# A pause between indirect gathers on GpSimd in place of a lock to the run sums, in a graph and mixture-of-experts layer

## Chip, cores and metric

The kernel runs on one core of one Trainium2 chip. The metric is the device time of one execution in microseconds (us). The time before is the median of three runs.

## What is computed

There are 6250 nodes of 256 float32 features, a first graph of 200,000 edges sorted by their target `dst`, and a second graph of 131,072 edges for a gate that picks two of four experts. Cut to what matters:

```python
x = x + gnn(_layernorm(x), W, M, src, dst)
x = x + ffn(_layernorm(x)[None], ...)[0]

def gnn(x, W, M, edge_src, edge_dst):
    self_term = x @ W
    msg = x @ M
    agg = segment_sum(msg[edge_src], edge_dst, num_segments=x.shape[0])
    return relu(self_term + agg)
# ffn: graph attention over edge_index gives scores (B, N, 4); top 2 are weighted by softmax;
#      out += g[..., None] * (gelu(x @ W1[e] + b1[e]) @ W2[e] + b2[e]) for e in range(4)
```

## The kernel before

The change lies in the first graph. The message product is taken after the sum, so what has to be summed over edges is the normalized `x` itself, kept in DRAM as `xn_d`. The sorted edges are cut into 1611 **visits** (`V_`): one visit is 128 edges whose targets lie in one tile of 128 nodes. For each visit j

- GpSimd (POOL in the profile) issues an indirect gather that fetches the 128 source rows of 1 KB each from `xn_d` into one slot of `ring` (line 1703);
- TensorE (PE) multiplies the slot by a 128 x 128 `one_hot` matrix of local targets, made on VectorE (line 752), which sums the rows by target in PSUM (line 1505);
- VectorE (DVE) adds that sum to the running sum of the tile and writes it back over the slot (line 818). This is `run`, with its place in VectorE's count of steps, `dve_at["run", j]`. The PE may be three visits ahead of it, no more: the matmul of visit j waits for `run` of visit j - 3.

`ring` has `RING = 4` parts of `JC = 8` slots. Eight visits are a **chunk**. When a chunk's run sums are done, the queue of SyncE (SP) stores it to `run_d` (line 1885), on a semaphore `stored{s}` of its part. TensorE waits at the start of a chunk until all eight gathers of it have landed. GpSimd may begin the gathers of chunk c when the chunk four places back is stored and the run sum of visit 8(c - 3) is done, so at most 24 visits ahead of the run sums. Before the change a second rule is in force: every even gather j waits also for the run sum of visit j - 14 (`LEAD = 14`).

Between visits, TensorE, VectorE and ScalarE (ACT) do other work in an order written out by hand and counted by visits: the sort of the second graph's edges (`sort_after`), the experts' matmuls (`unit_after`), and per tile of nodes the layer's product, its norm and its gate features (`due`). SP's queue moves the tiles of those. So a visit that comes later moves all of them. GpSimd does nothing but gathers in this stage. After the last visit GpSimd scatters the starts of the second graph's segments, and the second graph, which takes the rest of the time, begins.

Of the kernel before, what the change touches and what calls it, by code (L numbers as in the profile page):

```python
# [3 lines left out]
F32 = mybir.dt.float32  # L4
# [8 lines left out]
P = 128  # L13
# [14 lines left out]
UNIT_LAG = 2  # L28
LATE = 2
EARLY_STARTS = 27  # L30
LEAD = 14

TC = 32
WIDE_CHUNKS = 3
# [31 lines left out]
def sent(k):  # L66

    return 16 * (k + 1)


def build(nc, x, src, dst, W, M, W_gat, att_src, att_dst, b_gat, ln_gamma, ln_beta,
# [81 lines left out]
    r = Region(base)  # L153
# [20 lines left out]
    shift1 = r.take("shift1", [P, P], F32)  # L174
    up1 = r.take("up1", [P, P], F32)
    wrap1 = r.take("wrap1", [P, P], F32)
    node_id = r.take("node_id", [P, NT], F32)
    node_ii = r.take("node_ii", [P, NT], I32)
    row_at = r.take("row_at", [P, 1], I32)
# [135 lines left out]
    V, S, T, G, Q = nc.vector, nc.scalar, nc.tensor, nc.gpsimd, nc.sync  # L315
# [3 lines left out]
    def sem(name):  # L319
        if name not in named:  # L320
            named[name] = nc.alloc_semaphore(name)
        return named[name]

    dve_step = sem("dve_step")
    dve_at = {}

    def at_rows(ap):
        return bass.IndirectOffsetOnAxis(ap=ap, axis=0)
# [35 lines left out]
    def size(c):  # L364

        return max(0, min(JC, V_ - c * JC))
# [1293 lines left out]
    def gpsimd_program():  # L1660
# [32 lines left out]
        for c in range(NCH):  # L1693
            s = c % RING
            if c * JC % P == 0:
                G.wait_ge(sem("sources"), c * JC // P + 1)
            if c >= RING:
                G.wait_ge(sem(f"stored{s}"), sent(c // RING - 1))
                G.wait_ge(dve_step, dve_at["run", (c - RING + 1) * JC])
            for j in range(c * JC, c * JC + size(c)):  # L1700
                if j % 2 == 0 and j >= LEAD:
                    G.wait_ge(dve_step, dve_at["run", j - LEAD])
                G.indirect_dma_start(out=ring[:, s, j % JC, :], out_offset=None, in_=xn_d,  # L1703
                                     in_offset=at_rows(srci[:, j:j + 1])).then_inc(sem(f"gather{s}"), 16)

# [25 lines left out]
        for c in range(NCF):  # L1731
# [3 lines left out]
            for k in range(pool_cols[c]):  # L1735
                j = c * FC + k
# [250 lines left out]
    scalar_program()  # L1987
    tensor_program()
    gpsimd_program()
    sync_program()  # L1990

# [21 lines left out]
```

## Time and profile before

| what | value |
|---|---|
| median of 3 runs | 4055.15 us (4053.32 to 4062.95) |
| the profiled execution, its own time | 4024.76 us |
| its span, first to last instruction | 4023.5 us |
| granted TensorE clock, mean | 0.823 of full speed |
| first and last gather of the first graph | start at 63.8 and 2525.2 us |
| POOL gathers of the first graph | 1611, mean 973 ns |
| POOL busy over the span | 2164.3 us (54%) |

The first graph's visits fill 2461 us of the span (63.8 to 2525.2), over 60% of it. A group row gives the busy time of all its instructions, the mean time of one, and after the second bar the idle time of its engine right before them with what ended it. On POOL, spans of an instruction are rough, so the distance from start to start is the surer figure. "Issue" is idle time that no semaphore of the profile ended. PE and PEld (weight loads) are two rows of one engine, so their waits overlap.

### The profile page before, as it was taken

To read this page: it belongs to the slowest core of one execution; us is meant where nothing else is said; L and a number is where in the kernel's file an instruction comes from. 1 tells how busy PE (TensorE), PEld (TensorE's weight loads), DVE (VectorE), ACT (ScalarE), POOL (GpSimd) and SP (SyncE) were. 2 spreads that over 40 slices of the span, in tenths; PEclk is the share of its full clock that TensorE was granted. 3 is DMA by queue.
4 is the path that set the end of the run, shared out by engine and by line. 5 is a ranking of instruction groups with operands and counts; after the bars stand their busy time and mean duration, and the time that the engine had idled before them with its cause. 6 is when DMAs were issued, how large, how long until landed. Compare 5 with 4: busy or idle time off the path is not lost. (4 is left out here: it accounts for less than half of the span.)

```text
span 4023.5 us, 43371 instructions
## 1 busy us (share of the span) xinstructions
PE 2676.5 (67%) x13459; PEld 1995.0 (50%) x13459; DVE 2157.3 (54%) x5820; ACT 903.1 (22%) x1563; POOL 2164.3 (54%) x2248
## 2 busy tenths in 40 slices
PE   2567867776677776877877877622694646555844
PEld 1344545554455455555555555401683535454844
DVE  6777667776655556554545555200263534344866
ACT  3001111111122221111111111100352423233633
POOL 4666666666666665666666666577014353534031
PEclk9767879898888888999899888755896867777978
DMA  9676656666666665666666666401221111111146
GB/s 298 207 253 189 195 182 201 202 195 190 191 202 198 194 191 173 206 204 199 209 195 208 209 202 194 112 13 14 64 70 27 45 27 32 39 26 36 44 138 203
DMA packets 476804, 601.22 MB, mean 149 GB/s; under 512 B 72486, under 2 KB 415390, under 8 KB 474526
## 3 DMA queue, kind: packets, MB, share of 16 engines
q1 hardware_dynamic: 378766, 375.94, 28.6%
q0 software_dynamic: 97216, 219.88, 20.0%
q10 hardware_dynamic: 592, 2.64, 0.2%
q8 instruction: 108, 1.77, 0.2%
q14 instruction: 122, 1.00, 0.1%
HBM read 313.06 MB, written 286.79 MB: 149 GB/s over the span
## 5 line engine op out<-in xcount | busy, mean ns | idle before, releaser
L1703 POOL DMA_INDIRECT ring<-xn_d,srci x1611 | 1567.2, 973 | 902.1 <-DVE ring L818 416.9
L1505 PE MATMUL wide<-ring,one_hot 128*128 128x256 f32 x3222 | 983.1, 442 | 470.5 <-DVE ring L818 351.7
L818 DVE SCALAR_TENSOR_TENSOR ring<-ring,same_v,wide 128x256 f32<-128x256 f32 x1610 | 770.3, 478 | 942.6 <-remote 405.9
L1505 PEld LDWEIGHTS wide<-ring,one_hot 128*128 128x128 f32 x3222 | 666.5, 218 | 740.8 <-DVE ring L818 318.4
L1611 PE MATMUL wide<-tab_parts,low_hot 128*128 128x208 bf16 x6288 | 659.9, 262 | 329.5 <-issue 308.7
L1737 POOL DMA_INDIRECT g<-tab_d,srt x500 | 480.8, 962 | 629.5 <-DMA sum_d<-g 480.4
L1611 PEld LDWEIGHTS wide<-tab_parts,low_hot 128*128 128x128 bf16 x6288 | 576.3, 100 | 413.2 <-issue 377.0
L1563 PE MATMUL wide<-w2s,hh 128*128 128x256 f32 x1568 | 424.8, 420 | 150.5 <-issue 88.5
L1563 PEld LDWEIGHTS wide<-w2s,hh 128*128 128x128 f32 x1568 | 335.5, 216 | 225.9 <-issue 102.8
L1553 PE MATMUL wide<-xt,w1s 128*128 128x512 f32 (+1 forms) x832 | 419.1, 631 | 41.2 <-ACT hh L1238 23.5
L1238 ACT ACTIVATE hh<-wide,b1c 128x512 f32<-128x512 f32 (+1 forms) x208 | 137.7, 663 | 1299.1 <-remote 627.3
L875 DVE TENSOR_TENSOR picked<-wide,high_hot 128x832 f32<-128x832 f32 x131 | 133.8, 1021 | 466.7 <-remote 380.5
L752 DVE TENSOR_SCALAR one_hot<-iota_f,dloc 128x128 f32<-128x128 f32 x1611 | 363.0, 304 | 6.2 <-remote 3.0
L1314 ACT ACTIVATE low_hot<-far_off,ones 128x512 bf16<-128x512 f16 x262 | 173.9, 711 | 488.8 <-remote 418.2
L1553 PEld LDWEIGHTS wide<-xt,w1s 128*128 128x128 f32 x832 | 174.5, 216 | 174.3 <-issue 132.6
L793 DVE TENSOR_TENSOR yo<-wide,b2b 128x256 f32<-128x256 f32 x196 | 82.2, 419 | 270.5 <-remote 169.0
L1308 ACT ACTIVATE far_off<-low_row,lane_n 128x512 f16<-128x512 f16 x262 | 172.5, 706 | 0.0
L880 DVE TENSOR_REDUCE g<-picked 128x64 f32<-128x832 f32 x131 | 133.7, 1020 | 4.5
L1204 ACT ACTIVATE signs<-wide,smt 128x512 bf16<-128x512 f32 x98 | 67.3, 687 | 295.5 <-remote 151.8
L1257 ACT ACTIVATE tin<-wide 128x512 f32<-128x512 f32 x49 | 29.2, 596 | 389.8 <-remote 238.6
L650 DVE TENSOR_TENSOR keys<-keys 128x512 f32<-128x512 f32 (+1 forms) x198 | 112.2, 566 | 0.0
L651 DVE TENSOR_TENSOR keys<-keys 128x512 f32<-128x512 f32 (+1 forms) x198 | 112.1, 566 | 0.0
(369 smaller groups left out, 1730.2 us busy)
## 6 DMA issues: line engine op xcount, KB each, us to landing
run_d<-ring SPq DMA_DIRECT2D x201, 1024.0 KB
ring<-xn_d,srci POOLq DMA_INDIRECT x1611
y_d<-yo SPq DMA_DIRECT2D x196, 128.0 KB
comb<-y_d SPq DMA_DIRECT2D x28, 896.0 KB, 10.5
low_row<-low_d SPq DMA_DIRECT2D x13, 1024.0 KB
sum_d<-g SPq DMA_DIRECT2D x15, 768.0 KB, 3.9
g<-tab_d,srt POOLq DMA_INDIRECT x500
xn_d<-ring SPq DMA_DIRECT2D x7, 896.0 KB, 7.0
```

What stands on the lines that cost most here:

```text
L752: dve_at["one_hot", b] = step(V.tensor_scalar(one_hot[:, b % 4, i, :], iota_f[:, :], dloc[:, 4 * b + i:4 * b + i + 1], None, ALU.is_equal))
L818: dve_at["run", j] = step(V.scalar_tensor_tensor(out=o, in0=ring[:, (j - 1) // JC % RING, (j - 1) % JC, :], scalar=same_v[:, j:j + 1], in1 ...
L875: dve_at["taken", b] = then(V.tensor_tensor(picked[:, :, :, :], wide[:, 4 + half:6 + half, :].rearrange("p c (k x) -> p (c k) x", k=2)[:, ...
L1238: A.activation(hh[:, i % 2, f, 0:n * P], bank[hidden_bank[nl]][:, 0:n * P], ACT.Gelu, bias=b1c[:, e, f:f + 1], scale=1.0).then_inc(sem("ge ...
L1308: A.activation(far_off[:, b % 2, i, :], low_row[:, c % 2, at:at + LOW], ACT.Abs, bias=lane_n[:, 3 - i:4 - i]).then_inc(sem("far_off"), 1)
L1314: A.activation(low_hot[:, b % 2, 3 - i, :], far_off[:, b % 2, i, :], ACT.Relu, bias=ones[:, 0:1], scale=-1.0).then_inc(sem("low_quarter"), 1)
L1505: T.matmul(wide[:, 4 + j // 2 % 2, j % 2 * D:(j % 2 + 1) * D], one_hot[:, j // 4 % 4, j % 4, :], ring[:, j // JC % RING, j % JC, :], start ...
L1553: mm = T.matmul(bank[hidden_bank[nl]][:, 0:n * P], w1s[:, e, k, f * P:(f + 1) * P], xt[:, c % 2, k, 0:n * P], start=(k == 0), stop=(k == K ...
L1563: mm = T.matmul(bank[y_bank[ny]][:, 0:D], hh[:, i % 2, k, f * P:(f + 1) * P], w2s[:, e, k, :], start=(k == 0), stop=(k == KF - 1))
L1611: mm = T.matmul(bank[4 + 2 * (b % 2) + i // 2][:, at:at + HX * HI], low_hot[:, b % 2, q_, i * P:(i + 1) * P], tab_parts[:, k, q_, :, :].re ...
L1703: G.indirect_dma_start(out=ring[:, s, j % JC, :], out_offset=None, in_=xn_d, in_offset=at_rows(srci[:, j:j + 1])).then_inc(sem(f"gather{s} ...
L1737: G.indirect_dma_start(out=g[:, s, k, :], out_offset=None, in_=tab_d, in_offset=at_rows(srt[:, j:j + 1])).then_inc(sem(f"feat_in{s}"), 16)
```

## The change

Before each of the 1611 gathers, GpSimd writes zeros to a new tile `pause` of 128 x 128 float32, which nothing reads. The wait of every even gather for the run sum fourteen visits back is removed. Each memset waits until the one before it has completed, a memset that stands in GpSimd's order ahead of the gather ahead of it. The rules of the ring (part stored, run sum 24 visits back) stay, and now hold the chunk's first memset.

```diff
-LEAD = 14
+PAUSE = 128
...
     wrap1 = r.take("wrap1", [P, P], F32)
+    pause = r.take("pause", [P, PAUSE], F32)
...
                 G.wait_ge(sem(f"stored{s}"), sent(c // RING - 1))
                 G.wait_ge(dve_step, dve_at["run", (c - RING + 1) * JC])
             for j in range(c * JC, c * JC + size(c)):
-                if j % 2 == 0 and j >= LEAD:
-                    G.wait_ge(dve_step, dve_at["run", j - LEAD])
+                if j >= 1:
+                    G.wait_ge(sem("paused"), j)
+                G.memset(pause[:, :], 0.0).then_inc(sem("paused"), 1)
                 G.indirect_dma_start(out=ring[:, s, j % JC, :], out_offset=None, in_=xn_d,
                                      in_offset=at_rows(srci[:, j:j + 1])).then_inc(sem(f"gather{s}"), 16)
```

The other engines' programs keep their instructions and their order. GpSimd's order before, at the start of the gathers: `pairs` is an earlier gather, `ring<-xn_d,srci` are the visits' gathers.

```order
L1689 DMA pairs<-pair_d,vis_at 128x256 x12
L1703 DMA ring<-xn_d,srci 128x256 [waits xn_out3,xn_out2,sources,xn_out1,xn_out0]
L1703 DMA ring<-xn_d,srci 128x256 x13
L1703 DMA ring<-xn_d,srci 128x256 [waits dve_step]
L1703 DMA ring<-xn_d,srci 128x256
L1703 DMA ring<-xn_d,srci 128x256 [waits dve_step]
```

Fourteen gathers stand without a wait on VectorE's count, and from then on every second one has one. In the changed kernel the same place of GpSimd's order reads:

```order
L1690 DMA pairs<-pair_d,vis_at 128x256 x12
L1704 MEMSET pause 128x128 [waits xn_out3,xn_out2,sources,xn_out1,xn_out0]
L1705 DMA ring<-xn_d,srci 128x256
L1704 MEMSET pause 128x128 [waits paused]
L1705 DMA ring<-xn_d,srci 128x256
```

Memset and gather alternate, and VectorE's count is no longer waited for. Further on in the changed kernel, at visit 32, where the first part of the ring is used again, GpSimd's order reads:

```order
L1704 MEMSET pause 128x128 [waits paused,dve_step,stored0]
L1705 DMA ring<-xn_d,srci 128x256
L1704 MEMSET pause 128x128 [waits paused]
L1705 DMA ring<-xn_d,srci 128x256
L1704 MEMSET pause 128x128 [waits paused]
```

The wait for the ring's part now stands once in eight gathers, on the memset, and is the only one on another engine.

## Rows read from the trace of the kernel before

**Rows 1.** The profile's page: busy times, then TensorE's clock and DMA by slices

```profile
span 4023.5 us, 43371 instructions
PE 2676.5 (67%) x13459; PEld 1995.0 (50%) x13459; DVE 2157.3 (54%) x5820; ACT 903.1 (22%) x1563; POOL 2164.3 (54%) x2248
POOL 4666666666666665666666666577014353534031
PEclk9767879898888888999899888755896867777978
DMA  9676656666666665666666666401221111111146
```

**Rows 2.** Busy time of each engine in the stretch of the visits

```profile
core 0: us, PE busy (x) PEld busy (x) DVE busy (x) ACT busy (x) POOL busy (x), PEclk, DMA share, GB/s
63.00:2530.00 2467.00, 1822.38 (x6506) 1285.69 (x6507) 1472.04 (x4375) 403.71 (x679) 1569.25 (x1614) 0.86 0.65 202
```

**Rows 3.** Groups of instructions on POOL: gathers, and the start's memsets of 128 columns

```profile
L1703 POOL DMA_INDIRECT ring<-xn_d,srci x1611 | 1567.2, 973 | 902.1 <-DVE ring L818 416.9 <-issue 394.0 <-DVE one_hot L752 58.6
L1672 POOL MEMSET ones<- 128x128 f32 x1 | 0.2, 199 | 0.0
L1671 POOL MEMSET up<- 128x128 f32 x1 | 0.2, 198 | 0.0
```

**Rows 4.** Timeline of POOL, gathers one behind another: start, us, idle before

```profile
165.60 1.14 POOL L1703 DMA_INDIRECT ring<-xn_d,srci  x1 [0.30 <-issue]
167.05 0.94 POOL L1703 DMA_INDIRECT ring<-xn_d,srci  x1 [0.30 <-issue]
168.30 0.94 POOL L1703 DMA_INDIRECT ring<-xn_d,srci  x1 [0.30 <-DVE ring L818]
169.55 1.19 POOL L1703 DMA_INDIRECT ring<-xn_d,srci  x1 [0.30 <-issue]
```

**Rows 5.** The gathers' line: duration (min/median/max, ns), first and last start

```profile
L1703 POOL DMA_INDIRECT ring<-xn_d,srci x1611: 942/949/1807, 63.8 to 2525.2; - x179
```

**Rows 6.** The gathers alone by stretches: length, busy (count), clock, DMA share, GB/s

```profile
63.00:205.00 142.00, 99.41 (x100) 0.79 0.76 245
205.00:353.00 148.00, 98.75 (x100) 0.68 0.74 233
353.00:660.00 307.00, 197.46 (x197) 0.86 0.62 190
2200.00:2530.00 330.00, 205.14 (x216) 0.88 0.67 204
```

**Rows 7.** The visits' matmul, L1505: what ended the idle time before it

```profile
  DVE ring L818: 670.1, 338
  issue: 304.5, 294
  DMA ring<-xn_d,srci: 135.2, 62
```

**Rows 8.** Waits of the whole core: who waited for whom, total, times, longest

```profile
PEld wide L1505 <- DMA ring<-xn_d,srci: 70.8, 36, 5.4
PE wide L1505 <- DMA ring<-xn_d,srci: 64.4, 26, 15.3
DVE ring L818 <- remote: 405.9, 102, 8.4
DVE ring L818 <- PE wide L1505: 326.0, 175, 8.5
```

**Rows 9.** VectorE's `one_hot` line, and four of them in the timeline

```profile
L752 DVE TENSOR_SCALAR one_hot<-iota_f,dloc x1611: 267/281/515, 67.0 to 2527.0; 128x128 f32<-128x128 f32 x179
L752 DVE TENSOR_SCALAR one_hot<-iota_f,dloc 128x128 f32<-128x128 f32 x1611 | 363.0, 304 | 6.2 <-remote 3.0
1701.60 0.90 DVE L752 TENSOR_SCALAR one_hot<-iota_f,dloc 128x128 f32<-128x128 f32 x4
```

## Prediction

> **What bounds the kernel now.** I read the page first: TensorE is busy 67% of the span, VectorE and GpSimd 54% each, the DMA engines about 0.6 in the first graph's part [rows 1]. Nothing there is full, so the stretch of the visits was read next: of 2467 us TensorE is busy 1822 (74%), VectorE 1472 (60%), GpSimd 1569 (64%), DMA 0.65 [rows 2]. The visits are a loop over three engines, and what it lacks must be looked for in its waits.
>
> GpSimd's row says how the 1611 gathers share their time: 1567.2 us busy and 902.1 idle before them [rows 3]. The timeline shows what that idle time is made of: even where GpSimd waits for no one there are 0.30 us between the end of one gather and the start of the next, so the shortest distance from start to start is 1.25 us (168.30 to 169.55) [rows 4]. 1611 x 0.30 = 483 us are this gap, and 902 - 483 = 419 us are real waiting, 0.26 us for each gather. Most of it is put down to the run sum, 416.9 us (of which each of its 305 times holds the gap of 0.30 too); the `one_hot` that is named after it counts on the same semaphore [rows 3]. GpSimd is therefore not the bound: it could do a gather in 0.973 + 0.30 = 1.27 us and is asked for one in (2525.2 - 63.8) / 1610 = 1.529 us [rows 5].
>
> Who asks? TensorE's idle time before the visits is 670.1 us for the run sum, 304.5 "issue", and only 135.2 for the gathers' data [rows 7]. That last figure adds two rows of one engine, 70.8 us before weight loads and 64.4 before matmuls [rows 8], which may overlap; so late data cost somewhere between 71 and 135 us of TensorE's time at the very most, and the loop between TensorE and VectorE costs several times that. VectorE in its turn waits 326.0 us for the visits' matmul and 405.9 for a release that the trace does not name [rows 8]. The two stand in each other's way, and a gather earlier or later changes that only through the 71 to 135 us.
>
> **The change, part by part.**
>
> *The lock goes.* It removes the 419 us of waiting, but not as time won: GpSimd's waiting is where the loop is slower than GpSimd. What it brings is lead. With the lock the last pair of gathers of a chunk (8c + 6 and 8c + 7) may start only when the run sum of visit 8c - 8 is done, while TensorE wants the chunk when about the run sum of 8c - 3 is done: five visits, 5 x 1.53 = 7.6 us, less two gathers (2.5 us), leave 5.1 us for the transfer, and less where TensorE catches up after a wait. Without it only the ring's rule is left, 24 visits back, checked once in eight gathers. The late data of 71 to 135 us should then nearly vanish. How much of it is won? TensorE set free there runs sooner into its wait for the run sum of three visits back, the largest wait it has (670.1). I take half of the smaller figure, 35 us; the bounds are 0 and 71.
>
> *The memset comes.* The trace has memsets of exactly this shape at the start, 198 and 199 ns each, one right behind the other with no idle time [rows 3]. None of them stands behind a gather, so the price there is bounded. From below it is 0: the 0.30 us gap might be GpSimd's preparation of the next gather, and the memset might run within it. From above it is 0.199 + 0.30 = 0.50 us, if each change between memset and gather costs a gap again. I take 0.199, added to both the gather and its gap, because the memset's row shows no gap of its own. The pace is then 0.973 + 0.30 + 0.199 = 1.472 us a gather, 1611 x 1.472 = 2371 us for all, against 2461 now. The memset eats 321 of the 419 us that the lock took; GpSimd keeps 90 us of slack, 4%. The wait for the memset before is met already, since that one ran ahead of a whole gather, and costs nothing. If the slack is gone, every further 0.01 us of pace costs 16 us.
>
> *The places where GpSimd is the bound all the same.* The first hundred gathers take 142 us and the second hundred 148 [rows 6], 1.42 and 1.48 us each; at 1.472 the first hundred take 5 us more, the second about as now. The first chunk of eight lands 8 x 0.2 = 1.6 us later. From 353 on the gathers run at 307 / 197 = 1.56 us, and at the end at 330 / 216 = 1.53 [rows 6], slower than the new pace, so the ring fills and GpSimd waits for stores. Together 7 us lost, bounds 2 and 15.
>
> *VectorE beside the memset.* A `one_hot` takes 281 ns in the median and 515 at most, 304 in the mean [rows 9]; gathers go from 949 in the median to 1807 [rows 5]. The two disturb each other already. 1611 more writes of GpSimd might stretch some VectorE instructions by a part of 0.2 us; if one in five is hit by 0.1 us that is 32 us of VectorE's time, of which its 40% of idle time hides most. I set 6 us, bounds 0 and 32.
>
> Sum, against the profiled execution's own 4024.76 us: -35 + 7 + 6 = -22, so 4003. The medians of the runs shown stand 1.0076 times above it, so 4055 x (4003 / 4025) = 4033 us. Everything after the last visit keeps its work and is moved as a whole.
>
> **The rivals.**
>
> *A, the data were never the bound (no change, 4055).* The 71 us come back as waits for the run sum, and the start's 7 us are hidden. For it: 670.1 us of such waits against 135.2, and 405.9 us on VectorE that no gather ends. Against it: one wait of a matmul for the data is 15.3 us long [rows 8], and such a wait moves everything behind it.
>
> *B, the pause makes GpSimd the bound (slower).* The point from which this decides is a pace of 1.529 us. `one_hot` fills 363.0 of 2461 us, 15% of the time, in packs of four that last 0.90 us [rows 9]. If a memset that meets such a pack is held until it ends, it waits 0.45 us in the mean, 0.15 x 0.45 = 0.07 us a gather, and the pace is 1.54: 1611 x 1.54 = 2481 us, 20 more than now. GpSimd still waits for the ring now and then, a tenth of today's waiting by my guess, 42 us, less the 35 won and with the 6 on VectorE: 20 + 42 - 35 + 6 = 33 more, about 4088. For it: single gathers of 1.14 and 1.19 us in rows [rows 4] show that GpSimd is held now and then. Against it: the mean of 973 is only 24 ns over the median, so gathers, four times as long, lose little by all of VectorE's work.
> The Trainium skill, SBUF — State Buffer, section Who interferes with whom, states the rule that would do this: VectorE in a mode with two ports and GpSimd share one pair of ports, and whoever comes second is blocked for the whole instruction. That the gathers' mean lies so close to their median speaks for a small effect.
>
> *C, a gap of 0.30 us before the memset as well as before the gather (much slower).* The pace is 0.973 + 0.30 + 0.199 + 0.30 = 1.77 us; 1611 x 1.77 = 2854, 393 us more than now, about 4450. For it: the gap of 0.30 stands before every gather, also where nothing is waited for. Against it: no memset has one.
>
> *D, the memset hides in the gap.* The pace stays near 1.27 us, nothing is lost at the start, GpSimd runs ahead until the ring is full, and the gain is 35 to 71 us, about 4010. Against it: gathers come in denser bursts than any now, on DMA engines that are 0.65 busy, and could delay the other transfers; then it is no gain at all.
>
> **How the numbers follow.** My forecast (4033, own range 4010 to 4048) has 0.45, A 0.20, B 0.17, C 0.06, D 0.12. From no change this measurement can tell about 0.3%, 12 us. Faster by more than that: most of the forecast (0.33), two thirds of D (0.08), a little of A (0.02), together 0.43. Slower: all of C (0.06), most of B (0.14), small parts of the others (0.06), 0.26. The same: the rest, 0.31. The range reaches from D and a full gain of 71 us with nothing lost to B at its dearer end with a pace of 1.55 (2497 us, 36 more, plus the ring's 42): 3990 to 4110. Outside it are C and what lies below, about 0.12.
>
> **What would show it.** In the changed kernel's trace: the distance from gather to gather in an undisturbed stretch at 1.45 to 1.50 us (D: 1.27, C: 1.75); memsets of about 199 ns; TensorE's wait for the gathers' data down from 135.2 to under 30 us, after the first 200 us; GpSimd waiting mostly once in eight, for the store or the run sum; the last gather's start near 2505 us. Wrong I would be if distances above 1.53 fill the stretch and GpSimd hardly waits for anyone (B), or if the wait for data falls and the wait for the run sum grows by as much (A). A change in how long VectorE waits for what the trace does not name (405.9 us) would mean that the spacing of the gathers acts on something that I have not priced.

## The result and the profile after

The changed kernel is slower: 4263.89 us in the median of four runs (4257.78 to 4281.76) against 4059.05 us (4053.32 to 4069.32) for the kernel before in the same round, a ratio of 1.0509 (95% interval 1.0468 to 1.055). The forecast was 4033 us, and 4264 lies outside its range, between rivals B and C and by the mechanism of neither. The profiled execution of the changed kernel took 4269.35 us.

The page of the changed kernel, its busy times and the rows of slices:

```profile
span 4268.1 us, 44957 instructions
PE 2691.5 (63%) x13434; PEld 2006.0 (47%) x13459; DVE 2159.6 (51%) x5820; ACT 904.4 (21%) x1563; POOL 2540.3 (60%) x3859
POOL 5777777777776766676677677567502535353121
PEclk9667988797887888888888888875598677768878
DMA  9576565565564655555565556621131111111146
```

Beside [rows 1], no engine became fuller except GpSimd, whose 376 us more are nearly all memsets (368.9). TensorE, VectorE and ScalarE do the same work in a longer time. The slices, each 107 us long here and 101 before, keep their shape: the visits end in the 26th in both. What lies behind the last gather takes 4268.1 - 2757.1 = 1511 us, and took 1498.

The groups on POOL and VectorE in the changed kernel: busy time, mean of one, then the idle time before them and what ended it:

```profile
L1705 POOL DMA_INDIRECT ring<-xn_d,srci x1611 | 1577.7, 979 | 282.4 <-issue 269.7 <-POOL pause L1704 9.6 <-DVE ring L819 1.3
L1704 POOL MEMSET pause<- 128x128 f32 x1611 | 368.9, 229 | 476.3 <-DMA run_d<-ring 426.8 <-issue 27.1 <-DVE one_hot L753 12.9
...
L819 DVE SCALAR_TENSOR_TENSOR ring<-ring,same_v,wide 128x256 f32<-128x256 f32 x1610 | 770.9, 479 | 1172.4 <-remote 602.2 <-PE wide L1506 362.7 <-issue 105.7
L753 DVE TENSOR_SCALAR one_hot<-iota_f,dloc 128x128 f32<-128x128 f32 x1611 | 364.8, 313 | 3.4 <-DVE keys L652 0.2
```

Against [rows 3] the gathers lost their wait for the run sum and kept only a short gap. What GpSimd waits for now is the ring's part, 426.8 us for the store `run_d` before the first memset of a chunk. So GpSimd still has time to spare, and it is not the bound.

The gathers' own line, duration, first and last start:

```profile
L1705 POOL DMA_INDIRECT ring<-xn_d,srci x1611: 954/955/6902, 63.8 to 2757.1; - x179
```

The last gather starts at 2757.1 us in place of 2525.2 [rows 5], 231.9 us later. That is nearly the whole difference of the two profiled executions, 4269.35 - 4024.76 = 244.6 us. A visit takes (2757.1 - 63.8) / 1610 = 1.673 us instead of 1.529.

The chain of waits of the whole core names the place, in the changed kernel:

```profile
DVE ring L819 <- remote: 602.2, 127, 14.3
DVE ring L819 <- PE wide L1506: 362.7, 193, 8.5
DVE ring L819 <- issue: 105.7, 40, 14.0
```

"Remote" is the profile's word for a release that it can't name. VectorE waits for it 602.2 us where it waited 405.9 [rows 8], 196.3 us more, half of it by more waits (127 for 102) and half by longer ones (14.3 us at most, 8.4 before). All of VectorE's idle time before the run sum went from 942.6 to 1172.4 us, 230 more, nearly the 231.9 that the stretch grew; the rest of it, 36.7 us, is waiting for the visits' matmul. When both kernels were run again (below), the split was less sharp: of a stretch 214 us longer, 126 us were the unnamed waits (458.9 to 584.8) and 61 us the waits for the matmul.

One of these waits, in the timelines of the changed kernel (start, duration, then the idle time before), first VectorE, then TensorE, then GpSimd:

```profile
1777.20 1.05 DVE L819 SCALAR_TENSOR_TENSOR ring<-ring,same_v,wide 128x256 f32<-128x256 f32 x2
1791.24 1.06 DVE L819 SCALAR_TENSOR_TENSOR ring<-ring,same_v,wide 128x256 f32<-128x256 f32 x2 [12.99 <-remote]
...
1778.40 1.10 PE L1506 MATMUL wide<-ring,one_hot 128*128 128x256 f32 x4 [0.30 <-DVE ring L819]
1792.37 2.08 PE L1506 MATMUL wide<-ring,one_hot 128*128 128x256 f32 x4 [12.86 <-issue]
...
1779.49 0.22 POOL L1704 MEMSET pause<- 128x128 f32 x1
1779.88 0.95 POOL L1705 DMA_INDIRECT ring<-xn_d,srci  x1 [0.17 <-issue]
1780.82 0.23 POOL L1704 MEMSET pause<- 128x128 f32 x1
1781.22 0.95 POOL L1705 DMA_INDIRECT ring<-xn_d,srci  x1 [0.17 <-issue]
...
1789.26 0.95 POOL L1705 DMA_INDIRECT ring<-xn_d,srci  x1 [0.17 <-issue]
1790.21 0.22 POOL L1704 MEMSET pause<- 128x128 f32 x1
1790.60 0.95 POOL L1705 DMA_INDIRECT ring<-xn_d,srci  x1 [0.17 <-issue]
```

The matmuls that VectorE needs are recorded as over at about 1779.5 us (their ends are modelled, so this is rough). VectorE sees it at 1791.24, and TensorE, three visits ahead, can't go on either. All that time GpSimd issues one gather every 1.34 us. I call such a wait a **hold**: work of TensorE that is over reaches its waiters microseconds late.

Could it be VectorE itself that is kept from starting, while the news is there? The trace says no. It also keeps the times at which semaphores were counted up. In this example the semaphore of the visits' matmuls, which only TensorE counts, is recorded at 1776.29 and then at 1791.22 us, and at least 600 of the 602.2 us end on a count of this semaphore. Not every count is recorded, but these times agree with VectorE's start. ScalarE has unnamed waits of its own, nearly all behind other semaphores that only TensorE counts (of the first row, 485.3 us lie in the visits' stretch; the second lies there whole):

```profile
ACT hh L1239 <- remote: 683.7, 52, 33.0
ACT signs L1205 <- remote: 248.2, 39, 13.4
```

Holds are in the kernel before too, but shorter. This is one of its timelines, VectorE and then GpSimd:

```profile
1712.50 2.23 DVE L818 SCALAR_TENSOR_TENSOR ring<-ring,same_v,wide 128x256 f32<-128x256 f32 x4 [4.96 <-remote]
...
1709.57 0.95 POOL L1703 DMA_INDIRECT ring<-xn_d,srci  x1 [0.30 <-issue]
1713.24 0.95 POOL L1703 DMA_INDIRECT ring<-xn_d,srci  x1 [2.73 <-DVE ring L818]
```

Here the lock did something that the prediction had not seen. No run sum is done during a hold, so GpSimd soon runs into the lock; it fell silent at 1710.52 us, and the hold ended at 1712.50. With the lock gone GpSimd may go on until the ring is full.

Does the silence end the hold? I counted the unnamed waits at the run sum of 3 us or more. In the two traces of the kernel before, 145 of 158 ended while GpSimd had been idle for more than 0.6 us, with about 2 us of idle time in the median. The count proves little, since the lock opens only when the hold is over; that nine in ten of these idle times lie between 1.1 and 2.6 us speaks for the silence. In the two traces of the changed kernel, 124 of 179 ended while gathers were still coming. So a silence may end a hold sooner, but a hold also ends without one.

### The profile page after: what moved, and what is told of

The parts are those of the page before. It is cut to its first block and busy times, and to the rows that moved or that the text cites. A ratio compares the mean times of both kernels' runs of the same rounds, so it can differ in the third digit from the quotient of the medians.

```text
span 4268.1 us, 44957 instructions
## 1 busy us (share of the span) xinstructions
PE 2691.5 (63%) x13434; PEld 2006.0 (47%) x13459; DVE 2159.6 (51%) x5820; ACT 904.4 (21%) x1563; POOL 2540.3 (60%) x3859
## 5 line engine op out<-in xcount | busy, mean ns | idle before, releaser
L819 DVE SCALAR_TENSOR_TENSOR ring<-ring,same_v,wide 128x256 f32<-128x256 f32 x1610 | 770.9, 479 | 1172.4 <-remote 602.2
L1506 PE MATMUL wide<-ring,one_hot 128*128 128x256 f32 x3222 | 991.8, 443 | 580.5 <-DVE ring L819 331.8
L1704 POOL MEMSET pause<- 128x128 f32 x1611 | 368.9, 229 | 476.3 <-DMA run_d<-ring 426.8
L753 DVE TENSOR_SCALAR one_hot<-iota_f,dloc 128x128 f32<-128x128 f32 x1611 | 364.8, 313 | 3.4 <-DVE keys L652 0.2
L651 DVE TENSOR_TENSOR keys<-keys 128x512 f32<-128x512 f32 (+1 forms) x198 | 112.2, 567 | 0.0
```

Of the source, the lines that this page charges most:

```text
L753: dve_at["one_hot", b] = step(V.tensor_scalar(one_hot[:, b % 4, i, :], iota_f[:, :], dloc[:, 4 * b + i:4 * b + i + 1], None, ALU.is_equal))
L819: dve_at["run", j] = step(V.scalar_tensor_tensor(out=o, in0=ring[:, (j - 1) // JC % RING, (j - 1) % JC, :], scalar=same_v[:, j:j + 1], in1 ...
L1506: T.matmul(wide[:, 4 + j // 2 % 2, j % 2 * D:(j % 2 + 1) * D], one_hot[:, j // 4 % 4, j % 4, :], ring[:, j // JC % RING, j % JC, :], start ...
L1704: G.memset(pause[:, :], 0.0).then_inc(sem("paused"), 1)
```

## Experiments

Three theories are named in the expectations. **H**: completions of TensorE are held back while gathers follow each other densely; the lock made GpSimd silent early, and its removal makes holds longer. **M**: the memsets are what costs time. **G**: where nothing is held back, GpSimd's pace decides. The last came with the first experiments, which met a chip that treats the very same kernel before quite differently: 3033.62 us in place of 4059. Where a number below has "3034" beside it, it is from this condition of the chip; "4060" is the other. All kernels that ran together met the same condition, and nothing in the kernels chose it; nor is it bound to the number of the chip, since a chip numbered 9 was met in each. The expectations of the first four runs were written for 4060 only, so these runs can't test them.

### The two parts apart, and the lock's length (condition 3034)

Neither lock nor memset:

```diff
-                if j % 2 == 0 and j >= LEAD:
-                    G.wait_ge(dve_step, dve_at["run", j - LEAD])
```

> No lock and no memset. Theory H (hold): now and then the completion of a visit's matmul reaches VectorE several microseconds late, and it does so for as long as gathers keep coming; the lock of fourteen places made GpSimd fall silent soon in such a stretch, and without it only the ring does. Then this kernel is about as slow as the changed one, 4200 to 4290 us, and VectorE's unnamed wait before the run sum is near 600 us as there (406 before). Theory M (memset): the memset, its semaphore or the port it shares with VectorE is what costs, and this kernel is back at 4055 us or below, 4010 to 4070.

Measured: 3001.06 us against 3033.62, ratio 0.9882 (0.9852 to 0.9912), faster by 1.2%.

Both, the kernel before with the memset ahead of each gather:

```diff
+PAUSE = 128
...
                 if j % 2 == 0 and j >= LEAD:
                     G.wait_ge(dve_step, dve_at["run", j - LEAD])
+                if j >= 1:
+                    G.wait_ge(sem("paused"), j)
+                G.memset(pause[:, :], 0.0).then_inc(sem("paused"), 1)
```

> The lock of before is kept and the memset of the changed kernel is added. Theory H: the silence comes back with the lock; the memset only makes the distance from gather to gather 1.34 instead of 1.25 us, so 4045 to 4085 us and VectorE's unnamed wait near 406 us. Theory M: the memset costs what it costs in the changed kernel, 4200 us or more.

Measured: 3177.06 us, ratio 1.046 (1.0428 to 1.0492).

The lock at ten visits and at twenty, no memset:

```diff
-LEAD = 14
+LEAD = 10
```

> The kernel before with the lock at 10 places in place of 14. Theory H: GpSimd falls silent four visits sooner, so the held completions get shorter (VectorE's unnamed wait from 406 down to 300 to 370 us, none over 7 us), but the chunk's data come late (its last pair may start only when three visits before the chunk's first matmul are left): TensorE's wait for gathers rises from 135 to over 250 us; together 4050 to 4180. If the depth of the lock had nothing to do with the held completions, the unnamed wait stays at 400 us or above.

Measured: 3759.08 us, ratio 1.2383 (1.2345 to 1.2421).

```diff
-LEAD = 14
+LEAD = 20
```

> The kernel before with the lock at 20 places. Theory H: GpSimd goes on for six more gathers in a held stretch, so the longest wait of VectorE grows from 8.4 us towards 12, the sum from 406 to 480 to 560 us, and the time lies between the two kernels, 4090 to 4200 us. Theory M: with no memset the lock's depth matters little, 4030 to 4065 us.

Measured: 3003.41 us, ratio 0.9893 (0.9863 to 0.9923), the same as without a lock.

Waits and the gathers' line (duration, first and last start) of the run with neither, and then the same of the run with a lock of ten:

```profile
PE wide L1505 <- DMA ring<-xn_d,srci: 198.2, 84, 15.5
DVE ring L818 <- PE wide L1505: 443.9, 289, 7.0
L1701 POOL DMA_INDIRECT ring<-xn_d,srci x1611: 940/946/7559, 63.9 to 2135.3; - x179
```

```profile
PE wide L1505 <- DMA ring<-xn_d,srci: 833.5, 195, 15.3
L1703 POOL DMA_INDIRECT ring<-xn_d,srci x1611: 940/946/1726, 64.0 to 2893.7; - x179
```

With neither, there is no wait for "remote" at the run sum. A visit takes (2135.3 - 63.9) / 1610 = 1.287 us, hardly more than GpSimd's shortest distance of 1.25: here GpSimd is the bound, as theory G has it, and TensorE's matmuls wait 198 us for data. A lock of ten is too tight even here (833.5 us of waits for data), so the length of the lock matters very much on the side where the transfer has no room.

The groups on POOL of the run with both:

```profile
L1708 POOL DMA_INDIRECT ring<-xn_d,srci x1611 | 1581.4, 982 | 281.0 <-issue 133.1 <-POOL pause L1707 121.4 <-DVE ring L820 10.9
L1707 POOL MEMSET pause<- 128x128 f32 x1611 | 369.8, 230 | 25.7 <-DVE ring L820 18.0 <-ACT srci L1200 6.5 <-DVE ring L817 0.5
```

GpSimd waits 25.7 us before its memsets, so it never rests and the lock hardly acts. Against the run with neither the memset costs 3177 - 3001 = 176 us, 0.109 us a gather: its price where GpSimd is the bound.

### The changed kernel again, with one column and with 512 (condition 4060)

The two kernels once more, unchanged, beside the two with other widths:

> The changed kernel itself, beside the kernel before. The first job ran where the kernel before takes 3034 us and no completion of a matmul is held back; there the kernel with neither took 3001 and the one with both 3177. Theory G (GpSimd's pace, which the memset sets to 1.34 us a gather, bounds the visits once nothing else holds them): where before is near 3034 this is 3120 to 3180. Theory H (completions held as long as gathers keep coming): where before is near 4055 this is 4230 to 4290 again, and the time goes into waits that the trace does not name.

Measured: 4276.37 us (4253.33 to 4293.18), ratio 1.0504 (1.0464 to 1.0545).

> The kernel before, unchanged, for its trace on the chip of this job: either near 3034 us with no wait of VectorE before the run sum that the trace leaves unnamed, or near 4055 us with about 400 us of them.

Measured: 4058.57 us, ratio 0.9995 (0.9974 to 1.0016).

```diff
-PAUSE = 128
+PAUSE = 1
```

> The changed kernel with a memset of 1 column in place of 128. Theory G: a memset of one column took 0.10 us at the start of the trace against 0.20, and up to 0.17 us of a memset hide in the gap of 0.30, so the pace falls back to 1.25 to 1.27 us; where before is near 3034 this is 2995 to 3030, as the kernel with neither lock nor memset. Theory H: where before is near 4055 the columns do not matter and this is 4200 to 4290.

Measured: 4415.41 us (4377.15 to 4430.5), ratio 1.0847 (1.078 to 1.0914).

```diff
-PAUSE = 128
+PAUSE = 512
```

> The changed kernel with a memset of 512 columns. From 128 to 1 column the trace's start has 0.199 and 0.10 us, so 0.08 us for each 100 columns; 384 more are 0.30 us and the pace is 1.64 us. Theory G: 1611 x 0.30 = 480 us more than the changed kernel where before is near 3034, 3600 to 3680. Theory H: where before is near 4055 the gathers stand further apart than the visits ask for (1.53), GpSimd is the bound at 1.64 and the time is 4230 to 4330, little above the changed kernel, and the unnamed waits are smaller.

Measured: 4296.68 us, ratio 1.0573 (1.0536 to 1.0611).

The waits of VectorE at the run sum, in the kernel before, with one column, and with 512 columns (there with TensorE's wait for data, and the gathers' line):

```profile
DVE ring L818 <- remote: 458.9, 124, 8.2
DVE ring L818 <- PE wide L1505: 341.2, 165, 8.2
```

```profile
DVE ring L819 <- remote: 709.9, 130, 18.7
DVE ring L819 <- PE wide L1506: 331.4, 164, 13.4
DVE ring L819 <- issue: 141.6, 45, 14.8
```

```profile
DVE ring L819 <- PE wide L1506: 947.5, 377, 9.1
PE wide L1506 <- DMA ring<-xn_d,srci: 747.4, 169, 19.1
L1705 POOL DMA_INDIRECT ring<-xn_d,srci x1611: 951/952/6588, 64.0 to 2789.1; - x179
```

And the timeline of GpSimd with one column:

```profile
1703.64 0.12 POOL L1704 MEMSET pause<- 128x1 f32 x1
1703.95 0.95 POOL L1705 DMA_INDIRECT ring<-xn_d,srci  x1 [0.19 <-issue]
1704.90 0.11 POOL L1704 MEMSET pause<- 128x1 f32 x1
1705.20 0.94 POOL L1705 DMA_INDIRECT ring<-xn_d,srci  x1 [0.19 <-issue]
```

With one column the distance is 1705.20 - 1703.95 = 1.25 us: this memset costs no time at all, as it lies within the gap. So the run is close to the kernel with only the lock removed, and it is the slowest of the four, 4415.41 - 4062.52 = 353 us over the kernel before beside it. That is the sharpest finding: the memset's length isn't what costs, because taking nearly all of it away makes the kernel worse. It points to the removal of the lock, but doesn't isolate it. Every kernel without the lock that met condition 4060 still has 1611 memsets with their semaphore, and theory M counts the semaphore in; a kernel without lock and without memset was never met there. Theory H in its own words missed this run too, since it expected that the columns don't matter, 4200 to 4290 us. The memset of 128 columns is worth 4415 - 4276 = 139 us against one of 1 column. The waits for "remote" move with it: longest 8.2 us with the lock at a distance of 1.25, 18.7 without it at 1.25, 14.3 and 15.3 in the two traces of the changed kernel, without it at 1.34.

With 512 columns the unnamed waits at the run sum are nearly gone (13.7 us in all), although GpSimd does not stop for longer than the memset between two gathers. The time is no better, since now GpSimd is the bound: (2789.1 - 64.0) / 1610 = 1.693 us a visit, and TensorE waits 747.4 us for data. So holds can be avoided without a long silence. Whether it is the shortest distance of 1.66 us that does it, or that a GpSimd which is the bound is never far ahead, these runs don't separate.

### Distance against silence (these and all that follow met condition 3034)

The changed kernel with 256 columns:

```diff
-PAUSE = 128
+PAUSE = 256
```

> The changed kernel with a memset of 256 columns in place of 128, no lock. By the mean times of the memset at 128 and 512 columns (226 and 548 ns) the gathers then start 1.34 + 0.11 = 1.45 us apart, 2336 us for 1611. Where the kernel before takes about 4060 us (chips on which TensorE's completions are held back): if an even distance of 1.45 us is enough to keep completions from being held back (theory H with the threshold between 1.34 and 1.45), VectorE's unnamed wait at the run sum falls below 100 us, as with 512 columns (13.7 us), the visits go at 1.45 us each and the time is about 3930 to 4000 us, faster than before. If the threshold lies between 1.45 and 1.67, the unnamed wait stays at 500 us or more and the time is 4200 to 4280 us. Theory M (memsets are the cost) says slower than the changed kernel, 4300 or more. Where before takes about 3034 us nothing is held back and GpSimd's pace decides (theory G): 3034 + (1.45 - 1.29) x 1611 = about 3290 us.

Measured: 3319.04 us, ratio 1.0915 (1.0897 to 1.0933).

Three memsets of 512 columns ahead of every eighth gather:

```diff
-PAUSE = 128
+PAUSE = 512
...
-                if j >= 1:
-                    G.wait_ge(sem("paused"), j)
-                G.memset(pause[:, :], 0.0).then_inc(sem("paused"), 1)
+                for k in range(3 if j % 8 == 0 else 0):
+                    if j + k:
+                        G.wait_ge(sem("paused"), j // 8 * 3 + k)
+                    G.memset(pause[:, :], 0.0).then_inc(sem("paused"), 1)
```

> No lock, and three memsets of 512 columns ahead of every eighth gather only: seven gathers follow each other at 1.25 us, then GpSimd is silent for some 1.6 us longer, a mean of about 1.46 us, as with 256 columns at each gather. It tells an even distance from silences. If what releases held completions is a silence of GpSimd (theory S), this is better than 256 columns at each gather: unnamed waits of at most some 8 us each, and a time near or below before, 4000 to 4070 us, where before takes about 4060. If it is the even distance that counts (theory H), seven gathers at 1.25 us hold completions as one column did, and the time is between 4150 and 4400 us. Where before takes about 3034 us: about 3290 us by both.

Measured: 3307.07 us, ratio 1.0884 (1.0865 to 1.0902).

The kernels with neither and with both, again, for the other condition, which they didn't meet:

> The kernel before without the lock and without a memset. Where before takes about 4060 us, theory H (the lock made GpSimd silent early, and without it completions are held for as long as gathers follow at 1.25 us) says 4400 us or more, as one column did, with an unnamed wait at the run sum of 650 us or more; a theory that only the memset costs time says 4055 or less. Where before takes about 3034 us: 3001 us again, by both.

Measured: 2996.31 us, ratio 0.986 (0.9844 to 0.9877).

> Lock of fourteen visits and the memset of 128 columns. Where before takes about 4060 us: theory H, by which the lock ends each hold after eight to fourteen gathers, says the unnamed wait stays near before's 400 to 460 us or falls, and the time is 4030 to 4110 us; if the lock is of no account and the memset costs the time, about 4260 as the changed kernel. Where before takes about 3034 us: 3177 us again.

Measured: 3176.87 us, ratio 1.0447 (1.043 to 1.0465).

> The changed kernel with 256 columns, no lock; gathers at least 1.45 us apart. Where before takes about 3034 us: 3319 us again. Where before takes about 4060 us: if an even distance of 1.45 us already ends the held completions (theory H, threshold between 1.34 and 1.45), VectorE's unnamed wait at the run sum is below 100 us and the time is about 3930 to 4000 us; if the threshold lies between 1.45 and 1.67, the unnamed wait is 400 us or more and the time 4200 to 4280 us.

Measured: 3314.38 us, ratio 1.0929 (1.0895 to 1.0964).

> The kernel before without lock and memset. Where before takes about 3034 us: 3000 us again. Where before takes about 4060 us: theory H says 4400 us or more, an unnamed wait at the run sum of 650 us or more; if only the memset costs time, 4055 or less.

Measured: 2999.58 us, ratio 0.9881 (0.9849 to 0.9912).

> Lock and memset of 128 columns. Where before takes about 3034 us: 3177 us again. Where before takes about 4060 us: theory H, by which the lock makes GpSimd silent soon after a hold begins, says 4030 to 4110 us and an unnamed wait at the run sum of 460 us or less; if the lock is of no account and the memset costs the time, about 4260 us.

Measured: 3175.15 us, ratio 1.046 (1.0428 to 1.0492).

> Lock and memset of 128 columns. Where before takes about 3034 us: 3177 us again. Where before takes about 4060 us: theory H, by which the lock makes GpSimd silent soon after a hold begins, says 4030 to 4110 us and an unnamed wait at the run sum of 460 us or less; if the lock is of no account and the memset costs the time, about 4260 us.

Measured: 3175.21 us, ratio 1.0431 (1.0404 to 1.0459).

> The changed kernel with 256 columns, no lock. Where before takes about 3034 us: 3317 us again. Where before takes about 4060 us: if an even distance of 1.45 us ends the held completions, the unnamed wait at the run sum is below 100 us and the time about 3930 to 4000 us; if not, the unnamed wait is 400 us or more and the time 4200 to 4280 us.

Measured: 3318.65 us, ratio 1.0914 (1.0885 to 1.0944).

> Lock and memset of 128 columns, a last time. Where before takes about 3034 us: 3177 us again. Where before takes about 4060 us: theory H, by which the lock makes GpSimd silent soon after a hold begins, says 4030 to 4110 us and an unnamed wait at the run sum of 460 us or less; if the lock is of no account and the memset costs the time, about 4260 us.

Measured: 3179.42 us, ratio 1.0472 (1.045 to 1.0493).

The groups on POOL with 256 columns:

```profile
L1705 POOL DMA_INDIRECT ring<-xn_d,srci x1611 | 1581.9, 982 | 274.8 <-issue 241.6 <-POOL pause L1704 18.1 <-DVE one_hot L753 6.1
L1704 POOL MEMSET pause<- 128x256 f32 x1611 | 538.1, 334 | 6.9 <-ACT srci L1199 6.1
```

All of them fit theory G for this condition and show nothing more; 3319 and 3307 us are a little above its 3290. GpSimd's pace sets the time, whether its pauses are even or bunched: 256 columns at each gather and three times 512 at each eighth are 12 us apart, at a mean distance of 1.484 and 1.478 us. What tells H's two forms apart (even distance, or silence, which one expectation calls theory S) stays unmeasured, and so do lock and memset together, and 256 columns, where before takes 4060 us.

## Why the prediction was wrong

**The lock goes: this step failed.** The prediction priced its removal as a pure gain of lead, -35 us with bounds 0 and 71, and gave no bound above nothing. The first half came true where the trace was taken: TensorE's waits for the gathers' data fell from 64.4 and 70.8 us [rows 8] to 20.2 and 5.4, of which 15.6 are the one wait for the very first chunk. In the waits of the changed kernel:

```profile
PE wide L1506 <- DMA ring<-xn_d,srci: 20.2, 3, 15.6
PEld wide L1506 <- DMA ring<-xn_d,srci: 5.4, 2, 4.3
```

But the 405.9 us of waits that the trace does not name were quoted, set aside, and mentioned only in the last sentence as something "that I have not priced". They were the largest releaser of VectorE at the run sum. The sum put them at no change; they grew by 196.3 us, and the visits' stretch by 231.9. In condition 4060 each of the kernels without the lock, whatever the width of its memset, is slower than before by 205 to 353 us. In condition 3034 the removal gains 33 to 43 us (3034 to 3001, 3039 to 2996). That this is near the forecast's 35 us is luck: there, without the lock, TensorE's matmuls still wait 198.2 us for data, which the forecast let vanish, and GpSimd is the bound, which the forecast denied.

**The memset comes: right in direction, mis-sized.** Taken was 0.199 us a gather, in full on top of the gap. Measured is a pace of 1.34 us instead of 1.25 (above, 1779.88 to 1781.22), 0.09 us; in the condition 3034 it is 0.109 in the mean. The memset itself takes 229 ns in the mean, and it stands right behind the gather with no idle time; the gap behind it shrinks from 0.30 to 0.17 us. So 0.13 us of it lie in the gap, and one column (0.12 us) lies in it wholly. The truth stands half-way between the forecast and rival D, and the distance of 1.34 us lies outside the 1.45 to 1.50 that the prediction named as its sign. C is refuted by the timeline (no gap before the memset).

**The places where GpSimd is the bound.** In the first 142 us the changed kernel starts 96 gathers in place of 100, in the next 148 us 89 in place of 100 [rows 6]. That is 15 gathers, about 20 us at their pace, above the bound of 15. Holds act here too: VectorE's unnamed waits in these 290 us are 61.2 us; in the kernel before they were 19.8.

**VectorE beside the memset.** `one_hot` went from 304 ns [rows 9] to 313 in the mean. Its instructions overlap each other, and the time that VectorE is busy with them rose only from 363.0 [rows 9] to 364.8 us. That 1.8 lies within the bounds of 0 and 32, below the 6 taken.

**The rivals.** A's form, gain returned as other waits, was in part the right kind: TensorE's data waits fell by 44 us (matmuls) and 65 us (weight loads), and VectorE's idle time before the run sum grew by 230, so that the sign changed. But A named TensorE's waits for the run sum, and those fell a little, from 351.7 to 331.8 us before matmuls. B did not happen, GpSimd still waits 426.8 us for the ring. D had the right sentence, "denser bursts than any now ... could delay the other transfers", but bounded it at no gain. What is delayed is not a transfer that the trace shows but the news that a matmul is done.

What is shown: in condition 4060 the kernels without the lock are slower, a longer memset loses less than one of 1 column, and the loss stands in VectorE's waits at the run sum, most of them for news of TensorE that comes late. What is argued only: that the lock's removal alone is the cause, since no kernel without lock and memset was met there, and that the lock helps by making GpSimd silent during a hold. The timelines and the 2 us above fit it, but most holds of the changed kernel ended while gathers were still coming. By what path a gather delays TensorE's completions stays open; nothing in the trace names it.

No version here beats both kernels in both conditions. In the condition 3034 leaving out the lock, or a lock of twenty, gains 1.1 to 1.4% on before; in the condition 4060 the nearest kernel to it (one column) loses 8.5%. No other length of the lock was met in condition 4060, and 256 columns, which might have been better in the second, costs 9.2% in the first.

## What to carry to other kernels

A wait that seems only to slow an engine down may also keep it from disturbing others; before a throttle is removed, the largest wait whose releaser the profile cannot name has to be priced on both sides, not set aside. Here a memset put between two gathers cost less than its own duration, because part of it took the place of the gap; measure distances from start to start, not durations. And such a kernel should be timed in both conditions: without the lock it was 1% faster in one, and with a memset of one column, the nearest to it, 8% slower in the other.

## What was not expected of the hardware

- The same kernel took about 4060 us at some times and 3034 at others, with the same instructions. No trace of it was kept where it takes 3034, but none of the other kernels' traces from there has a single wait for "remote"; where it takes 4060, 405.9 and 458.9 us of them stand at its run sum. In such a trace the visits' semaphore is also counted up fewer times than there are visits: 1225 recorded counts for 1611 matmuls in the kernel before, against 1608 in the run with neither in condition 3034. Whether counts come in bundles or records are missing, the trace doesn't tell. The visits' stretch of the kernel with the lock and no memset ends at 2558.5 us in the repeated run of the kernel before (condition 4060), 1511 us before its end; without the lock, in condition 3034, it ends at 2135.3 of 3000.9, 866 before the end. So the second graph, which gathers on GpSimd too, takes longer as well. The kernel before has unnamed waits there, 418.2 us on ScalarE (`low_hot`) and 380.5 on VectorE (`picked`), behind a semaphore that only TensorE counts.
- In condition 4060 news of finished matmuls came late: VectorE waited up to 15.3 us for it (18.7 with one column) while gathers were issued every 1.25 to 1.34 us, and in the example above it came some 11.7 us after the matmul's recorded end. With 512 columns, at 1.69 us a gather, VectorE waited 13.7 us for such news in the whole stretch.
- The memset's width reaches VectorE. `one_hot` takes 304 ns in the mean without a memset [rows 9], 313 with 128 columns, 356 with 256 (condition 3034) and 475 with 512. Its line (minimum, median and maximum in ns) in the changed kernel, and then in the one with 512 columns:

```profile
L753 DVE TENSOR_SCALAR one_hot<-iota_f,dloc x1611: 268/283/687, 67.0 to 2768.8; 128x128 f32<-128x128 f32 x179
```

```profile
L753 DVE TENSOR_SCALAR one_hot<-iota_f,dloc x1611: 266/495/844, 67.1 to 2782.4; 128x128 f32<-128x128 f32 x179
```

  The median moves from 283 to 495 ns, and the longest from 515 [rows 9] over 687 to 844. That is 329 ns more, less than the 548 of that memset. The Trainium skill, SBUF — State Buffer, section Who interferes with whom, has VectorE and GpSimd share a pair of ports in VectorE's modes that use both, the second to come being blocked; these rows agree in kind, with a mean rise of 9, 52 and 171 ns. That `one_hot` runs in such a mode no row shows.
- A memset of 128 columns alone takes 198 to 199 ns [rows 3], behind a gather 229 in the mean, and one of a single column 122 ns.
